# Two attention layers over 128 graphs: values and copy-out for two graphs at once, flips in halves, and k's low half padded by transfers within SBUF

## What is computed

```python
# layer 0: 8 heads of 32, scores masked where adj == 0
q, k, v = x @ Wq + bq, x @ Wk + bk, x @ Wv + bv
h = softmax(q @ k.T / sqrt(32) + mask0) @ v          # per graph and head
x = layernorm(h @ Wo + bo + x) * gamma + beta
# layer 1: adj is mask and edge weight alike
q, k, v = (ln(x) @ wq + bq), (ln(x) @ wk + bk), (ln(x) @ wv + bv)
x1 = x + softmax(q @ k.T / sqrt(32) + 0.1 * adj * adj + mask1) @ v @ wo + bo
out = x1 + gelu(ln(x1) @ w1 + b1) @ w2 + b2
```

## Time and profile before

| | us |
|---|---|
| median of three runs | 2339.82 (2336.93 to 2341.52) |
| the profiled execution | 2341.47 |
| its span, first to last instruction | 2339.7 |
| TensorE busy in it | 2217.5 |
| VectorE, ScalarE, GpSimd busy | 1867.4, 1848.4, 1619.8 |

### The profile page before, as it was taken

How to read it: one execution, slowest core, us unless ns; L and a number is a source line. 1 busy time by engine, 2 the same in 40 slices (tenths; PEclk the granted TensorE clock), 3 DMA queues, 4 the chain that set the end, 5 groups by cost and what they waited for, 6 DMA issues and landing times.

```text
span 2339.7 us, 58882 instructions
## 1 busy us (share of the span) xinstructions
PE 2217.5 (95%) x19008; PEld 1906.6 (81%) x19008; DVE 1867.4 (80%) x7045; ACT 1848.4 (79%) x5902; POOL 1619.8 (69%) x1165
## 2 busy tenths in 40 slices
PE   6789999999999999999999999999999999999987
PEld 5678888888888888888888888888888888888776
DVE  5798888888888789887889888889888879888741
ACT  4678889878888888888888888888888978888862
POOL 2567787667777677777677777676778676778742
PEclk7899999999999999999999999999999999999998
DMA  4001101101100101100101110101110101100000
GB/s 124 28 28 37 33 15 37 36 27 36 31 20 29 36 27 36 31 23 26 36 27 36 31 31 19 36 27 36 33 35 13 36 27 36 36 31 5 24 10 18
DMA packets 80767, 72.78 MB, mean 31 GB/s; under 512 B 3008, under 2 KB 72256, under 8 KB 80704
## 3 DMA queue, kind: packets, MB, share of 16 engines
q1 hardware_dynamic: 80704, 71.98, 10.1%
HBM read 55.20 MB, written 16.78 MB: 31 GB/s over the span
## 4 chain that ended last, share of the span: by engine, by line
PE 89%; DVE 4%; issue 4%; POOL 2%; ACT 1%; DMA 0%; DVEq 0%; POOLq 0%; SPq 0%; ACTq 0%
PE ps_j L414 62%; PE ps_s L374 10%; PE ps_t L390 8%; PE ps_o L406 6%; PE ps_j L425 3%; DVE pm L718 1%; DVE actl L748 1%; POOL pm L863 1%; ACT pm L531 0%; POOL hl L916 0%; PE ps_o L344 0%; POOL kp1l L871 0%; DVE stats L799 0%; DMA pm<-in_wv 0%; ACT kp0h L573 0%
## 5 line engine op out<-in xcount | busy, mean ns | idle before, releaser
L531 ACT ACTIVATE pm<-pm,nmax 128x128 f32<-128x128 f32 x2048 | 795.6, 398 | 81.0 <-DVE nmax L718 76.7
L863 POOL TENSOR_TENSOR pm<-pm,rinv 128x512 f32<-128x512 f32 x512 | 544.3, 1081 | 431.9 <-DVE rinv L729 431.8
L718 DVE CUSTOM_DVE_ANT_0 pm<-ps_s,m 128x128 f32<-128x128 f32 x2048 | 464.7, 284 | 58.0 <-PE ps_s L374 49.1
L531 ACT ACTIVATION_READ_ACCUMULATOR pm<-pm,nmax 128x1 f32 x2048 | 400.8, 196 | 0.0
L916 POOL TENSOR_TENSOR hl<-hf,hh 128x512 fp32r<-128x512 f32 x256 | 343.2, 1344 | 40.7 <-ACT hf L608 28.8
L390 PE MATMUL ps_t<-ident,pm 128*128 128x128 f32 x2048 | 275.7, 278 | 21.5 <-POOL pm L863 21.2
L414 PE MATMUL ps_j<-w2h,hh 128*128 128x256 f32 x1024 | 292.3, 285 | 2.8 <-POOL hl L916 2.8
L414 PE MATMUL ps_j<-w2h,hl 128*128 128x256 f32 x1024 | 288.3, 282 | 0.0
L414 PE MATMUL ps_j<-w2l,hh 128*128 128x256 f32 x1024 | 288.3, 282 | 0.0
L545 ACT ACTIVATE oth<-ps_o 128x256 fp32r<-128x256 f32 x256 | 98.8, 386 | 225.4 <-PE ps_o L406 225.2
L390 PEld LDWEIGHTS ps_t<-ident,pm 128*128 128x128 f32 x2048 | 231.3, 142 | 42.8 <-POOL pm L863 30.8
(11 more groups left out here) (148 smaller groups left out, 6726.8 us busy)
## 6 DMA issues: line engine op xcount, KB each, us to landing
xTr<-in_xT SPq DMA_DIRECT2D x32, 512.0 KB, 3.6
xy<-in_x SPq DMA_DIRECT2D x32, 512.0 KB, 4.0
out<-x SPq DMA_DIRECT2D x32, 512.0 KB, 2.9
m<-in_adj SPq DMA_DIRECT2D x32, 256.0 KB, 2.8
a<-in_adj SPq DMA_DIRECT2D x32, 256.0 KB, 4.2
r<-in_wo SPq DMA_DIRECT2D x2, 256.0 KB, 6.5
x<-in_w SPq DMA_DIRECT2D x1, 512.0 KB, 9.0
v<-in_w SPq DMA_DIRECT2D x1, 512.0 KB, 7.5
```

Source lines behind the costliest of these rows:

```text
L531: last = nc.scalar.activation(pm[:, g % 2, h, :], pm[:, g % 2, h, :], ACT.Exp, bias=nmax[:, g % 2, h:h + 1], scale=-1.0, accum_out=rsum[:, ...
L718: last = nc.vector.tensor_tensor_reduce(out=pm[:, g % 2, h, :], in0=ps_s[c][:, j * N:(j + 1) * N], in1=m[:, g, :], scale=1.0, scalar=3e38, ...
L863: tt(pm[:, g % 2, hs, :], pm[:, g % 2, hs, :], rinv[:, g % 2, hs].rearrange("p (h a) -> p h a", a=1).to_broadcast([P, HC, N]), ALU.mult).t ...
```

## The change

Six edits are made together.

- `values` now takes two graphs (`half` 0 or 1) and fills the whole bank `ps_o`; `out_hi` and `out_lo` copy 512 columns instead of 256, half as often. `values` waits once for `ot_lo` of the half before, and for the copies of each of its two graphs.
- `flip` takes one half (4 heads) per call, so that other work can be put between the two.
- `pad_k` leaves GpSimd. `kp[l][1]` is set to zero once at the start (two memsets on POOL), and for each chunk SP issues four transfers of 32 rows x 512 columns (64 KB each) from `hf` into the places that aren't zero. That is 16 transfers an iteration.
- The wait of `scores` at `g = 0` is on those transfers, by a semaphore for each chunk.
- `JOBS` and the bodies of all engines are reordered, and where an iteration begins is moved.
- `qk_lo` writes `hf` in the other type name, with the same bits.

```diff
+            def pad_k(l, b, n):          # SP
+                c = n % C
+                if exists(b):
+                    if isinstance(b, int) and b == 0:
+                        sp.wait_ge(kp_zero, 2)
+                    taken(sp, b, f"QKV{l}", n)
+                    for j in range(HC):
+                        rows = slice(j * HD, (j + 1) * HD)
+                        sp.dma_start(kp[l][1][rows, c, j % 2, :].bitcast(F32), hf[rows, c, :]).then_inc(kp_lo[l][c], 16)
...
             def body(i):
-                load_xT(i + 1); store(i - 3); load_x(i); load_adj1(i); load_adj0(i + 1)
+                load_xT(i + 1); store(i - 3); load_x(i); load_adj1(i); load_adj0(i + 1); pad_k(Y, i - 1, 2)
+                pad_k(Y, i - 1, 3); pad_k(X, i + 1, 2); pad_k(X, i + 1, 3)
 
             iterate(sp, body, {FIRST: load_first, 0: load_rest})
...
-            def pad_k(l, b, n):          # POOL
-                c = n % C
-                if exists(b):
-                    taken(pool, b, f"QKV{l}", n)
-                    tt(kp[l][1][:, c, :, :], hf[:, c:c + 1, :].to_broadcast([P, 2, T]),
...
+            for l in (0, 1):
+                nc.gpsimd.memset(kp[l][1][:, :, :, :].bitcast(F32), 0.0).then_inc(kp_zero, 1)
...
+            def values(l, b, half):
+                if exists(b):
...
+                    before = earlier(l, b, half, 1, 2)
+                    if before:
+                        pe.wait_ge(ot_lo[before[0]], 2 * before[1] + before[2] + 1)
+                    for g in (2 * half, 2 * half + 1):
+                        pe.wait_ge(pt_a[l], slot(b, g) + 1)
+                        pe.wait_ge(pt_b[l], slot(b, g) + 1)
+                        for h in range(H):
...
-                qkv(Y, i - 1, 1); qkv(Y, i - 1, 2); flip(X, i, 1); qkv(Y, i - 1, 3); scores(X, i, 3); values(X, i, 0)
-                qkv(Y, i - 1, 4); flip(X, i, 2); qkv(Y, i - 1, 5); flip_rows("T2", i - 2, 0); values(X, i, 1)
-                flip_rows("T2", i - 2, 1); scores(Y, i - 1, 0); values(X, i, 2); flip(X, i, 3); mlp_up(i - 2, 0)
+                qkv(Y, i - 2, 0); qkv(Y, i - 2, 1); qkv(Y, i - 2, 2); flip(X, i - 1, 1, 0); flip(X, i - 1, 1, 1)
+                qkv(Y, i - 2, 3); scores(X, i - 1, 3); values(X, i - 1, 0); qkv(Y, i - 2, 4); qkv(Y, i - 2, 5)
+                flip(X, i - 1, 2, 0); flip(X, i - 1, 2, 1); flip_rows("T2", i - 3, 0); flip_rows("T2", i - 3, 1)
+                scores(Y, i - 2, 0); flip(X, i - 1, 3, 0); mlp_up(i - 3, 0); mlp_up(i - 3, 1); flip(X, i - 1, 3, 1)
...
-                mask_scores(Y, i - 2, 0, 1); out_lo(X, i - 1, 2); mask0(i); copy_pt(X, i - 1, 3)
+                norm_stats(0, i - 1); qk_lo(X, i, 0); mask_scores(Y, i - 2, 2, 0); qk_lo(X, i, 1); recip(Y, i - 2, 1)
...
+                copy_pt(X, i, 3); mask_scores(Y, i - 1, 1, 0); mask_scores(Y, i - 1, 1, 1); recip(Y, i - 1, 0)
+                out_lo(X, i, 1); x_lo(i + 1, 0); x_lo(i + 1, 1); residual("WO0", i, 0); residual("WO0", i, 1)
+                mask0(i + 1)
```

More of the change, by code:

```diff
@@ L74, in slot, with earlier @@
     return b * G + g
-def earlier(l, b, g, k):
+def earlier(l, b, g, k, n=G):
     while True:
@@ L186, in program @@
         qk_hi = [sem(f"qk_hi{l}") for l in (0, 1)]
-        kp_lo = [sem(f"kp_lo{l}") for l in (0, 1)]
+        kp_zero = sem("kp_zero")
+        kp_lo = [[sem(f"kp_lo{l}{c}") for c in range(C)] for l in (0, 1)]
         xb_done = sem("xb_done")
@@ L363, in scores @@
                     if g == 0:
-                        pe.wait_ge(kp_lo[l], C * (b + 1))
+                        for c in range(C):
+                            pe.wait_ge(kp_lo[l][c], 16 * HC * (b + 1))
                     before = earlier(l, b, g, 1)
@@ L380, in scores, with flip @@
                         second_products()
-            def flip(l, b, g):
+            def flip(l, b, g, c):
                 if exists(b):
[L384 to L392, removed]
@@ L394, in values @@
-            def values(l, b, g):
-                if exists(b):
[L396 to L400, removed]
+                    pe.wait_ge(norm_done[l], 2 * slot(b, g) + c + 1)
                     before = earlier(l, b, g, 1)
                     if before:
[L403 to L407, removed]
+                        pe.wait_ge((pt_a, pt_b)[c][before[0]], slot(*before[1:]) + 1)
@@ new lines, in flip @@
+                    for j in range(HC):
+                        last = nc.tensor.transpose(ps_t[c][:, j * N:(j + 1) * N],
+                                                   pm[:, g % 2, c * HC + j, :], ident[:, :])
+                    last.then_inc(pt_full[l], 1)
+            def values(l, b, half):
+                if exists(b):
+                    if half == 0:
+                        taken(pe, b, f"QKV{l}", 5)
+                    before = earlier(l, b, half, 1, 2)
[5 more added lines that the diff above has]
+                        for h in range(H):
+                            j, at = h % HC, (h // HC) * 2 * N + g % 2 * N
+                            last = mm(ps_o[j * HD:(j + 1) * HD, at:at + N],
+                                      v[l][:, g, h * HD:(h + 1) * HD], pt[:, g % 2, place(h), :], start=True, stop=True)
@@ L481, in body @@
             def body(i):
[L482 to L486, removed]
@@ L492, in body @@
-                mlp_up(i - 2, 4); mlp_up(i - 2, 5); mlp_up(i - 2, 6); mlp_up(i - 2, 7); out_proj(X, i, 0)
+                flip(X, i - 1, 0, 0); flip(X, i - 1, 0, 1); scores(X, i - 1, 2); out_proj(Y, i - 3, 1)
+                qkv(Y, i - 2, 0); qkv(Y, i - 2, 1); qkv(Y, i - 2, 2); flip(X, i - 1, 1, 0); flip(X, i - 1, 1, 1)
+                qkv(Y, i - 2, 3); scores(X, i - 1, 3); values(X, i - 1, 0); qkv(Y, i - 2, 4); qkv(Y, i - 2, 5)
+                flip(X, i - 1, 2, 0); flip(X, i - 1, 2, 1); flip_rows("T2", i - 3, 0); flip_rows("T2", i - 3, 1)
@@ new lines, in body @@
+                scores(Y, i - 2, 0); flip(X, i - 1, 3, 0); mlp_up(i - 3, 0); mlp_up(i - 3, 1); flip(X, i - 1, 3, 1)
+                scores(Y, i - 2, 1); values(X, i - 1, 1); mlp_up(i - 3, 2); mlp_up(i - 3, 3); mlp_up(i - 3, 4)
+                mlp_up(i - 3, 5); mlp_up(i - 3, 6); mlp_up(i - 3, 7); out_proj(X, i - 1, 0); out_proj(X, i - 1, 1)
+                flip(Y, i - 2, 0, 0); flip(Y, i - 2, 0, 1); qkv(X, i, 0); qkv(X, i, 1); scores(Y, i - 2, 2)
+                qkv(X, i, 2); qkv(X, i, 3); mlp_down(i - 3, 0); qkv(X, i, 4); flip(Y, i - 2, 1, 0)
@@ L494, in _ @@
+                flip(Y, i - 2, 1, 1); scores(Y, i - 2, 3); values(Y, i - 2, 0); mlp_down(i - 3, 1)
+                flip(Y, i - 2, 2, 0); mlp_down(i - 3, 2); flip(Y, i - 2, 2, 1); scores(X, i, 0); mlp_down(i - 3, 3)
+                flip(Y, i - 2, 3, 0); qkv(X, i, 5); flip(Y, i - 2, 3, 1); flip_rows("T1", i - 1, 0); scores(X, i, 1)
+                values(Y, i - 2, 1); flip_rows("T1", i - 1, 1); out_proj(Y, i - 2, 0)
             iterate(pe, body, {FIRST: first_weights})
```

96 lines of the change are left out of this document (43 added, 53 removed), and 10 rows, old and new, of the table JOBS.

## The result

| | us |
|---|---|
| changed kernel, median of 4 runs | 2456.17 (2451.51 to 2458.63) |
| kernel before, beside it, median of 4 | 2340.43 (2336.93 to 2341.52) |
| ratio | 1.0495, 95% interval 1.0475 to 1.0515 |
| the profiled execution | 2451.51, span 2449.6 |

What follows compares the result with a forecast made beforehand. TensorE's own stream plus its waits was taken as the bound. Terms -42 - 7 - 19 + 90 + 17 = +39 us on 2341.5 gave 2380.5, predicted as a median of 2379 us, range 2346 to 2410.

Steps and rivals of the forecast that it cites:

- the price of the wait: Before scores(Y, 0), TensorE waits 2.9 us per block for layer 1's k paddings: 31 x 2.9 = +90 us.
- The 0.25 before the first `mlp_up`: TensorE's wait between T2's transposes and that job, 0.25 us per iteration, goes: -7 us.
- The gain from fewer turns: TensorE's own stream: fewer switches between kinds of work save 0.6 us an iteration, -19 us (bounds 0 and -29).
- the wait before `values`: TensorE's 1.57 us wait per iteration for copy_pt behind mask0 vanishes as mask0 moves to the body's end: -42 us.
- Turning is free: Rival, chance 0.12: TensorE's stream gains nothing from fewer switches, the -19 is missing: 2398 us.
- The start: Program start: load_rest behind block 0's paddings delays the weights and first normalisation: +17 us (bounds +14 and +20).
- SP's pitch: Spacing of SP's successive padding issues, taken as 0.50 us (0.37 plus 0.05 at the quick end).
- the landing: Time for a 64 KB padding to land, taken as 2.2 us (ends 1.5 and 2.8).
- the likeliest case: Whole kernel: slower, chance 0.62, own range 2352 (wait 2.3, start +14) to 2402 (wait 3.5, start +20).
- VectorE became late behind x: Rival, chance 0.10: mask0 still costs 2.48, delaying qk_lo(X) and TensorE's qkv(X) jobs: up to +56, 2435 us.
- the 0.42 counted: mask0 on VectorE in its new place at the body's end, with GpSimd mostly idle: 0.42 us.
- The paddings land in time: Rival, chance 0.10: quicker issues and landing shorten the wait before scores(Y, 0); with none, -51, 2289 us.

Runs made afterwards that it cites:

- 12 fillers: Changed kernel plus 12 extra 256-column matmuls on constant weights before the wait for the paddings in scores(Y), except block 0's: 2390.84 us (1.0226).
- with 24: Changed kernel plus 24 extra 256-column matmuls on constant weights before the wait for the paddings in scores(Y), except block 0's: 2387.14 us (1.0195).

## Why the prediction was wrong

**The step that failed** is the price of the wait: "So TensorE waits 2.9 us in every block", and then "31 x 2.9 = +90 us". The wait was found and measured at 2.88, but it was priced one to one. It costs 2.1 us more each time, because TensorE works at 1.2 GHz behind it. The term should have been 31 x 5.0, about +155. I read the clock as something that doesn't change: the kernel before had only waits of up to 1.8 us in the loop, at a mean clock of 1.00. But its clock did fall in four iterations, and the same rows hinted at it: one iteration took 69.53 us and the mean of all was 69.82. Besides, the sum put new small waits at nothing.

The loop's period by terms: 70.3 forecast, 73.17 measured. The clock is 2.1 of the difference. Another 0.7 is in small waits: 3.60 of idle time where 2.9 were counted. TensorE's own stream came to the period forecast, but by luck, as the next paragraph shows. The 0.25 before the first `mlp_up` went, as forecast, but T2's own transposes now wait 0.23 for `norm_rows(2)`. A flip waits 0.34 for `normalise`, and a job 0.37 in two iterations of three for `hf`.

**The gain from fewer turns** was put at 0.6 us an iteration. The busy time did fall by 0.55 (68.00 in the earlier trace rows against 1753.58 / 26 = 67.45), but about 0.25 of that is the clock that no longer falls in four iterations: the other 22 of the kernel before have 67.8. So 0.3 is left, half of what was counted. No run tells whether it comes from the turns; with the same `values` and flips and the paddings on GpSimd, the run that measured 2338.81 has 67.95 over its 26 periods, which is more than before. "Turning is free" is neither shown nor refuted.

**Right:** the wait before `values` vanished. The start came to 17 (125.1 against 108.3 for the first `scores(Y, 0)`; 20 by experiment). **Right by two errors that cancel:** the wait of 2.9. I took 0.50 for SP's pitch and 2.2 for the landing; the pitch is 0.62 (4.96 us for eight) and the landing 2.0. So `scores(Y, 0)` started 9.4 us after the end of `scores(X, 3)` (1344.74) and not 8.7, but TensorE was ready after 6.5 us and not 5.8. One slip changes nothing: by its own terms the likeliest case reaches down to 2379 - 19 - 3 = 2357, and not to 2352.

**The rivals.** VectorE became late behind x only a little: `mask0` took 1.10 us in the mean, more than the 0.42 counted and less than the 2.48 feared, and the wait of a `qkv(X)` job for `hf` is 6.7 us in the loop where up to 56 were feared. "The paddings land in time" was false for this kernel, but its mechanism is what the experiments used: with one load moved, they nearly do (0.36 of waiting is left). The result is 2304 without the loss at the start; the rival's 2289 held 17 us for that, so it would be 2272 here.

## What to carry to other kernels

- A wait of the bounding engine isn't priced by its length alone. Compare its busy time for the same instruction count, and the granted clock behind the wait; here 2.9 us of waiting cost 5.
- In a queue that serves in order, look for the entry whose own wait holds back those behind it. One load moved behind eight small transfers turned 4% slower into 1.5% faster.
- A step taken off an engine also changes whom its neighbours meet: putting the paddings back on GpSimd in an order made without them cost as much as the transfers did.

## What the runs showed of the hardware

- TensorE's granted clock fell to 0.5 in every iteration of the loop with a wait of 2.9 us, for most of 7 us in the block shown, and in 4 of 26 with a wait of 1.57 (the kernel before). With 12 fillers it stayed at 1.00 beside waits of 1.34 us in every iteration, and with 24 at no wait, with the same transfers in flight. With the paddings on GpSimd it fell behind 13 of 17 waits of 2.6 us and behind 6 of 1.4.
- A 64 KB transfer within SBUF, 32 rows x 2 KB, landed 2.0 us after its issue, and four of them followed each other at 0.62 us on SP's queue. With 128 KB it landed at 2.4 us, or at 3.0 when an adjacency load had been issued just ahead.
- The same VectorE subtraction of 128x512 took 1.1 us or 2.1 in the mean of two runs; within the slower one it took 0.68 us with GpSimd idle and 4.6 beside four of GpSimd's instructions.
